# Every 64th (in the last stage every 32nd) gather of a graph kernel left out by GpSimd and fetched row by row from other queues

## What is computed

```python
h = relu(layernorm(x)); x = x + gcn(h)          # segment_sum(weight * (h W)[src], dst)
h = relu(layernorm(x)); x = x + hyperbolic(h)   # per edge: distance, 2-layer gate, h[col] * gate, segment_sum over row
h = relu(layernorm(x)); x = x + three attention layers(h)
    # e = leaky(alpha_s[src] + alpha_d[dst]); softmax over the edges of a node; segment_sum(h[src] * alpha, dst)
h = relu(layernorm(x)); x = x + two relational layers(h)
    # mean over the edges of each (dst, relation), times that relation's 64x64 matrix, summed
```

## Time and profile before

| | us |
|---|---|
| median of 3 runs | 17307.61 (17297.01 to 17308.78) |
| the profiled execution | 17330.74 |
| its span (first to last instruction) | 17329.0 |
| hyperbolic gathers, first to last start | 3252.8 to 5515.0 |
| attention gathers, three layers | 5779.3 to 12327.3 |
| last relational gathers | 15196.7 to 17296.0 |

### The profile page before, as it was taken

How to read it: one execution, slowest core, us unless ns; L and a number is a source line. 1 busy time by engine, 2 the same in 40 slices (tenths; PEclk the granted TensorE clock), 3 DMA queues, 4 the chain that set the end, 5 groups by cost and what they waited for, 6 DMA issues and landing times. The chain is left out here.

```text
span 17329.0 us, 347894 instructions
## 1 busy us (share of the span) xinstructions
PE 12031.7 (69%) x77017; PEld 8971.5 (52%) x77018; DVE 12499.8 (72%) x30848; ACT 7380.6 (43%) x19204; POOL 11519.1 (66%) x11855
## 2 busy tenths in 40 slices
PE   4443338599997577777777777777777888844444
PEld 2222225466665466665666666666546565533333
DVE  7777769777777788887888878888766666634443
ACT  1111129555554566665666656666441222300000
POOL 2777750377775577776777767777307777777777
PEclk7555555677776555555556555655696777755555
DMA  6333344333335222223222232222494666511111
GB/s 235 96 93 94 93 93 123 109 102 103 102 102 90 73 58 58 58 58 73 58 58 58 58 78 58 58 58 58 161 381 126 180 185 178 176 45 26 26 26 32
DMA packets 1329349, 1689.67 MB, mean 98 GB/s; under 512 B 835210, under 2 KB 903562, under 8 KB 1296591
## 3 DMA queue, kind: packets, MB, share of 16 engines
q1 hardware_dynamic: 899089, 875.57, 17.4%
q0 software_dynamic: 412640, 597.16, 15.7%
q10 hardware_dynamic: 17474, 215.22, 3.3%
HBM read 1072.24 MB, written 618.81 MB: 98 GB/s over the span
## 5 line engine op out<-in xcount | busy, mean ns | idle before, releaser
L2166 POOL DMA_INDIRECT gat_from_src<-gat_src_dram,gat_src_at x4992 | 4821.8, 966 | 1680.6 <-issue 1520.8
L3213 PE MATMUL rel_ps_sum<-all_node,rel_msg 128*64 128x128 f32 x6656 | 1413.5, 383 | 1501.4 <-DVEq L3172 1471.3
L3027 POOL DMA_INDIRECT rel_from_src<-typed_dram,rel_src_at x1664 | 1651.1, 992 | 1079.7 <-ACT rel_src_at L3042 596.7
L2387 PE MATMUL gat_ps_sum<-all_node,gat_msg 128*80 128x128 f32 x9984 | 2266.1, 420 | 42.3 <-DVE gat_msg L2281 7.9
L3213 PEld LDWEIGHTS rel_ps_sum<-all_node,rel_msg 128*64 128x64 f32 x6656 | 1133.8, 199 | 1979.2 <-DVEq L3172 1230.3
L1630 POOL DMA_INDIRECT all_node<-hyp_dst_dram,hyp_src_at x1768 | 1724.9, 976 | 603.0 <-issue 513.3
L2387 PEld LDWEIGHTS gat_ps_sum<-all_node,gat_msg 128*80 128x80 f32 x9984 | 2057.5, 252 | 102.3 <-issue 42.7
L3027 POOL DMA_INDIRECT rel_from_src<-typed_next_dram,rel_src_at x1664 | 1593.3, 958 | 566.2 <-issue 493.0
L1094 POOL DMA_INDIRECT bucket_dram<-all_node,order_index x1664 | 1616.0, 971 | 524.3 <-issue 505.8
L2329 DVE TENSOR_TENSOR again_sums_x<-again_sums_x,gat_ps_sum 80x128 f32 x4992 | 1393.1, 279 | 385.4 <-DVE again_sums_x L2329 213.0
L2291 DVE TENSOR_TENSOR_SCAN gat_ps_log<-gat_masks,gat_top,gat_ps_log 8x1024 f32<-8x1024 bf16 x624 | 1461.9, 2343 | 228.3 <-DVE again_sums_x L2329 220.4
(11 more groups left out here) (571 smaller groups left out, 26929.1 us busy)
## 6 DMA issues: line engine op xcount, KB each, us to landing
typed_dram<-typed_res SPq DMA_DIRECT2D x98, 2080.0 KB, 7.2
typed_next_dram<-rel_res ACTq DMA_DIRECT2D x98, 2080.0 KB
gat_relrow<-in_rows_dram SPq DMA_DIRECT2D x624, 256.0 KB
all_node<-gcn_table_dram SPq DMA_DIRECT2D x1664, 48.0 KB
gat_from_src<-gat_src_dram,gat_src_at POOLq DMA_INDIRECT x4992
bucket_dram<-by_dst_zero POOLq DMA_DIRECT2D x48, 1326.0 KB, 6.6
gsum_rec<-bucket_dram SPq DMA_DIRECT2D x221, 288.0 KB, 2.8
all_node<-lo_rows_dram SPq DMA_DIRECT2D x221, 256.0 KB
```

Of the source, the lines that this page charges most:

```text
L2166: nc.gpsimd.indirect_dma_start(from_src[:, q, k, :], None, g.gat_src[:, :], bass.IndirectOffsetOnAxis(ap=src_at[:, q, k:k + 1], axis=0)).t ...
L2387: last = nc.tensor.matmul(ps_sum[0:rows, k, :], msg[:, q % 2, k, :], member[:, q, k, :], start=True, stop=True)
L3027: nc.gpsimd.indirect_dma_start(from_src[:, q, k, :], None, table[:, :], bass.IndirectOffsetOnAxis(ap=src_at[:, q, k:k + 1], axis=0)).then_ ...
L3213: last = nc.tensor.matmul(ps_sum[0:D, k, :], msg[:, q % 2, k, :], member[:, q, k, :], start=True, stop=True)
```

## The change

**Which tiles.** In the three attention layers and the hyperbolic loop the eighth tile of every eighth chunk (one gather of 64), in the last relational layer the eighth tile of every fourth chunk (one of 32) is no longer gathered by GpSimd. It gathers seven tiles for these chunks. In the hyperbolic loop this is done for the 27 full groups of eight chunks. The first relational layer is as before.

**How they come instead.** SyncE reads 16 indices of that tile into registers (one TENSOR_LOAD, L211) and issues 16 one-row DMAs (L221) into a buffer `side` of 128 rows, once for each chunk, so that a group of eight chunks brings 128 rows. In the last layer a group has four chunks, and ScalarE issues 16 rows of each chunk beside the 16 of SyncE. At the last chunk of a group SyncE waits until all 128 rows have landed and the slot of the ring is free, and copies `side` into the ring with one DMA (`relay`). The next group's first fetch waits until that copy has landed, on ScalarE too. The consumers wait for it beside their seven gathers.

**With it.** The loops of SyncE, GpSimd and VectorE in attention and of all but TensorE in the hyperbolic stage are written for eight chunks instead of four (`eights`); the two mask loads of a chunk become one; the index rows for the fetches are loaded ahead of each loop (in the last layer converted by two VectorE copies of one partition, for which SyncE and ScalarE wait); in the stage of the GCN sums one transposition, one copy and two small stores make the index rows for the hyperbolic loop; in `typed_tables` TensorE waits for the weights after its first 25 transpositions and not before them.

The core of the diff:

```diff
+def fetch_piece(nc, eng, engine, rows, table, index, c, at, landed, top):
+    regs = bases(nc, engine, index, c, count=PIECE, per=PIECE, top=top)
+    for e, reg in enumerate(regs):
+        eng.dma_start(rows[at + e:at + e + 1, :], table[ds(reg, 1), :]).then_inc(landed, 16)
...
@@ edges_attention, SyncE (the hyperbolic loop: the same, without masks)
+                def relay(c, r, i):
+                    if r == GROUP - 1:
+                        for h in range(2):
+                            sp.wait_ge(side_in[h], 16 * (P // 2) * (i + 1))
+                            alone(sp, mark_s)
+                        sp.wait_ge(filled, free4(c))
+                        alone(sp, mark_s)
+                        sp.dma_start(from_src[:, r % 4, K - 1, :], side[:, :]).then_inc(side_out, 16)
+
+                def fetch(c, r, i):
+                    if r == 0 and not (isinstance(i, int) and i == 0):
+                        sp.wait_ge(side_out, 16 * i)
+                        alone(sp, mark_s)
+                    fetch_piece(nc, sp, ENG.SP, side, g.gat_src, single, c, r * PIECE, side_in[r // 4], N)
...
-                    for n, m in enumerate((g.first_mask, g.last_mask)):
-                        sp.dma_start(masks[:, q, n, :], m[ds(c * CE, CE)].partition_broadcast(H)
-                                     ).then_inc(mask_in[q], 16)
+                    sp.dma_start(masks[:, q, :, :], g.masks[:, ds(c * CE, CE)].partition_broadcast(H)).then_inc(mask_in[q], 16)
...
-                rounds(sp, [(load_rows, 4), (load_masks, 3)])
+                eights(sp, [(load_rows, 4), (load_masks, 3), (relay, 4), (fetch, 5)])
...
@@ edges_attention, GpSimd
-                    for k in range(K):
+                    for k in range(K if r < GROUP - 1 else K - 1):
...
@@ edges_attention, VectorE
-                    dve.wait_ge(got[q], 16 * K * (i + 1))
+                    dve.wait_ge(got[r], 16 * (K if r < GROUP - 1 else K - 1) * (i + 1))
+                    if r == GROUP - 1:
+                        dve.wait_ge(side_out, 16 * (i + 1))
...
@@ edges_relational, last layer
+                    rounds(sp, [(relay, 4), (fetch(sp, ENG.SP, 0, mark_s), 5)])
...
-                    for k in range(K):
+                    for k in range(K if first or q < 3 else K - 1):
...
-                    slotted(act, [(fields, 4), (activate, None, LAG)])
+                    act.wait_ge(single_c, 2)
+                    slotted(act, [(fields, 4), (fetch(act, ENG.Activation, 1, mark_a), 5), (activate, None, LAG)])
...
@@ typed_tables, TensorE
-                pe.wait_ge(w_in, 48)
...
                 pe.wait_ge(flips.row_kept, FLIPS)
+                pe.wait_ge(w_in, 48)
```

More of the change, by code:

```diff
@@ L55 @@
 ROW = 3 * P + 4
+PIECE = 16
+GROUP = P // PIECE
+SIDES = BCHUNKS // GROUP
 LAG = 16
@@ L146, in rounds, with eights, turn, in_fours @@
         turn(t, t // 4, t % 4)
+def eights(eng, steps, count=CHUNKS, full=None):
+    def turn(t, i, r):
+        for step, lead in steps:
+            if not isinstance(t, int) or 0 <= t + lead < count:
+                step(t + lead, (r + lead) % GROUP, i + (r + lead) // GROUP)
+    for t in range(-max(lead for _, lead in steps), 0):
+        turn(t, t // GROUP, t % GROUP)
+    full = (count - max(lead for _, lead in steps)) // GROUP if full is None else full
+    with eng.Fori(0, full) as i:
+        for r in range(GROUP):
+            turn(i * GROUP + r, i, r)
+    for t in range(GROUP * full, count):
+        turn(t, t // GROUP, t % GROUP)
+def in_fours(*steps):
+    def four(step):
+        return lambda c, r, i: step(c, r % 4, i * (GROUP // 4) + r // 4)
+    return [(four(step), lead) for step, lead in steps]
 def slotted(eng, steps, count=CHUNKS, slots=OWN_TILES):
@@ L328, in _ @@
                 sp.wait_ge(stored, 1)
-                for n, m in enumerate((g.first_mask, g.last_mask)):
+                for n in range(2):
+                    m = g.masks[n]
                     sp.dma_start(m[0:EP].rearrange("(g p e) -> p g e", p=P, e=P), mask[:, n, :, :]).then_inc(loaded, 16)
@@ L1414, in _ @@
                              ).then_inc(stored, 16)
-                sp.wait_ge(stored, 32)
+                sp.wait_ge(copied, len(tiles) + 1)
+                for h, row in enumerate(g.single_hyp):
+                    sp.dma_start(row.rearrange("o (j e) -> o j e", e=D), asides[0:SIDES, h * D:(h + 1) * D]).then_inc(stored, 16)
+                sp.wait_ge(stored, 64)
 def after_gcn(nc, g):
@@ L1619, in load, with gather @@
                     sp.dma_start(lorow[:, q % 2, :], g.lo_rows[ds(c * CE, CE)].partition_broadcast(P)).then_inc(lo_in[q], 16)
-                rounds(sp, [(load, 0)], BCHUNKS)
+                def relay(c, r, i):
[3 more added lines that the diff above has]
+                            alone(sp, mark_s)
+                        sp.wait_ge(joined, free4(c))
+                        alone(sp, mark_s)
+                        sp.wait_ge(h_kept, free4(c))
+                        alone(sp, mark_s)
+                        sp.dma_start(from_dst[:, r % 4, K - 1, :], side[:, :]).then_inc(side_out, 16)
+                def fetch(c, r, i):
+                    if isinstance(c, int) and c >= SIDES * GROUP:
+                        return
+                    if r == 0 and not (isinstance(i, int) and i == 0):
+                        sp.wait_ge(side_out, 16 * i)
+                        alone(sp, mark_s)
+                    fetch_piece(nc, sp, ENG.SP, side, g.hyp_dst, g.single_hyp[r * PIECE // D], i * GROUP // 2 + r % 4,
+                                r * PIECE, side_in[r // 4], N)
+                eights(sp, [*in_fours((load, 0)), (relay, 0), (fetch, 1)], BCHUNKS, full=SIDES - 1)
             @block.gpsimd
             def _(pool):
-                def gather(c, q, i):
+                def gather(c, r, i):
+                    q = r % 4
                     pool.wait_ge(joined, free4(c))
@@ L2980, in edges_relational, with fetch, step @@
             full, rest = N // P, N % P
+        def fetch(eng, engine, h, mark):
+            def step(c, q, i):
+                if q == 0 and not (isinstance(i, int) and i == 0):
+                    eng.wait_ge(side_out, 16 * i)
+                    alone(eng, mark)
+                fetch_piece(nc, eng, engine, side, table, single[h], c, h * D + q * PIECE, side_in[h][q // 2], top_row)
+            return step
         def place_of(engine, j, order, top):
@@ L3011, in _, with relay @@
                 else:
+                    for h in range(2):
+                        sp.dma_start(single[h].bitcast(F32).rearrange("o (c e) -> o c e", e=D),
+                                     g.tile_rows[:, h * D:(h + 1) * D].rearrange("(o c k) e -> o c k e", o=1, k=4 * K)[
+                                         :, :, 4 * K - 1, :]).then_inc(single_in, 16)
                     sp.dma_start(x[:, :, :], g.xs[:, :, :]).then_inc(x_in, 16)
+                    sp.wait_ge(single_c, 2)
+                    def relay(c, q, i):
+                        if q == 3:
+                            for landed in (*side_in[0], *side_in[1]):
+                                sp.wait_ge(landed, 16 * 2 * PIECE * (i + 1))
+                                alone(sp, mark_s)
+                            sp.wait_ge(filled, free4(c))
+                            alone(sp, mark_s)
+                            sp.dma_start(from_src[:, q, K - 1, :], side[:, :]).then_inc(side_out, 16)
+                    rounds(sp, [(relay, 4), (fetch(sp, ENG.SP, 0, mark_s), 5)])
                     sp.wait_ge(out_kept, START + OWN_TILES)
@@ L3149, in messages @@
                 def messages(c, q, i):
-                    dve.wait_ge(got[q], 16 * K * (i + 1))
+                    dve.wait_ge(got[q], 16 * (K if first or q < 3 else K - 1) * (i + 1))
+                    if not first and q == 3:
+                        dve.wait_ge(side_out, 16 * (i + 1))
                     dve.wait_ge(summed, half_ready(c, 1) - 4)
@@ L3185, in _ @@
                     dve.sem_inc(out_kept, START)
+                    dve.wait_ge(single_in, 32)
+                    for h in range(2):
+                        v.tensor_copy(single[h], single[h].bitcast(F32)).then_inc(single_c, 1)
                     dve.wait_ge(x_in, 16)
```

107 lines of the change are left out of this document (78 added, 29 removed).

## The result

The changed kernel takes **17252.1 us** (median of 9 runs, 17233.1 to 17269.5) against 17306.0 for the kernel before beside it (9 runs, 17296.0 to 17320.3): a ratio of 0.997, 95% interval 0.996 to 0.998, 54 us faster. The forecast was 17182 us, 126 us faster: right in sign, inside the range, and off by more than half of the gain. The profiled execution has a span of 17250.4 us, at its kernel's median, while the one shown for before lay 23 us above its own; so the two traces differ by 78.6 us where the medians differ by 54.

A forecast was written before the change was run, and what follows sets the result against it. GpSimd's gathers were taken to bound attention and the last stage, less surely the hyperbolic one. Attention -99, hyperbolic -35, last stage +8 and small parts 0 gave -126 us: 17307.6 to 17182 us, range 17090 to 17420.

The forecast's parts named there:

- Attention, -99 forecast: Attention layers: 78 gathers left out at 1.268 us each save 99 us, with GpSimd staying the bound.
- SyncE's sum of 76.8 us for a group: Attention: SyncE's rows, registers, loads, copy and landings take 76.8 us per eight chunks, against GpSimd's 79.9.
- a SyncE late by 10 us delays nobody, only its throughput counts: Attention: SyncE's waited-for signals come two chunks before their data are used, so 10 us of lateness costs nothing.
- Rival C: Attention: VectorE's longer loop fetches its code again each turn; three fetches make attention +265, 17546 us; chance 0.08.
- Hyperbolic, -35 forecast: Hyperbolic loop: 27 gathers left out at 1.280 us save 35 us; zero if TensorE's 91% is already its limit.
- Last stage, +8 forecast: Last relational layer: ScalarE takes over as bound at 40.5 us a group, +8 us instead of a 66 us gain.
- rival A: Last stage: ScalarE keeps up, so GpSimd stays the bound, -66 instead of +8, 17108 us; chance 0.30.
- half-difference of 0.027 us: Last stage: half the gap between ScalarE's 0.374 and SyncE's 0.320 us store, added to ScalarE's row, 0.48 us.
- Small parts, 0 forecast: Outside the main loops: `typed_tables` -14, last loop's start +10, hyperbolic index rows +2, attention starts +1 each; 0, within 15.
- The row price: SyncE's time per one-row DMA at a register address: 0.444 us, bounds 0.418 and 0.517.
- rival B: One-row issues cost as much as 128-partition ones, 0.517 us on SyncE and 0.571 on ScalarE: 18015 us; chance 0.19.
- the estimate of 0.464: Attention: a 72-float row, issued to 12 engines, might resemble the 8-partition mask load, 0.464 us in all.

The follow-up runs named there:

- Run 5: run 3 with SyncE fetching 8 of the 16 rows a chunk in attention, the other 64 edges getting fixed rows: 17148.9 us.
- run 3: The change with VectorE's attention loop and VectorE's and ScalarE's hyperbolic loops turning every four chunks instead of eight: 17217.5 us.
- run 7: run 6 with attention's 128 rows fetched in seven of a group's eight chunks, 17 to 19 rows each: 18327.8 us.
- run 9: run 6 with attention's 128 rows fetched in seven of a group's eight chunks, every register load of 16 as in the change: 17135.3 us.
- run 6: The change with VectorE's attention loop turning every four chunks and the hyperbolic stage as in the kernel before, without fetches: 17216.5 us.
- runs 4: The kernel before with VectorE's attention loop turning every eight chunks instead of four, nothing fetched or left out: 17320.6 us.
- Run 11: run 9 with VectorE's attention loop turning every eight chunks, as in the change: 17139.5 us.
- run 8: The kernel before with GpSimd gathering seven blocks a chunk in the hyperbolic stage, the eighth keeping 128 fixed rows: 17276.2 us.
- run 12: The kernel before with only the moved wait for the weights in `typed_tables`: 17292.3 us.
- runs 1: The kernel before with only the edits of `typed_tables` and the last relational stage; attention and hyperbolic stage untouched: 17228.8 us.

## Why the prediction was right in sign and wrong in size

**Attention, -99 forecast, +1 measured. The step that failed is SyncE's sum of 76.8 us for a group.** By the trace: rows 128 x 0.411 = 52.6 (I had 56.8), the rest of each chunk 8 x 2.49 = 19.9 (I had 16.8 for registers, destination and mask loads; the register load is 1.14, not 0.81, since I drew the price of a register from a load of eight on SyncE and one of one on ScalarE), 3.1 for the turn of the loop (I had put 0.8, and 2.5 to 2.8 of it is the code fetch), 3.0 for the copy and its landing (I had 2.4), and 1.4 for the rows that start later than that after the one before: 80.0 us; a whole turn in the third layer takes 80.4. That is above GpSimd's 79.9, so SyncE took the bound by a hair, and with it came the 7 to 9 us between the layers. I had the row itself too dear, what stands around it too cheap, and so the bound at the wrong engine: "a SyncE late by 10 us delays nobody, only its throughput counts" held inside the layers, and the throughput was what ran out; at the layers' ends the lateness was paid too. Run 5 (64 rows fewer, 60 us faster than run 3), run 7 (16 us more, 14 us a group) and run 9 (one landing hidden, 98 us faster than run 6) show it.

**Rival C stood beside the forecast with 0.08 and was a part of the cause.** Its mechanism came (2.7 to 2.9 us a turn at VectorE, where I had put 1.6 to 2.4), but I priced it at VectorE alone, whose slack takes it (runs 4 and 11), and left SyncE's own loop of 338 instructions out of the sum, although I named its length. Without its 2.5 us SyncE's turn would be some 78 us, under GpSimd's 79.9 (an estimate from the turn of 80.4); no run gives SyncE a short loop with all its rows, so how much of the loss is C's stays open. The earlier trace rows had only one of two instruction queues: q8 with 65 packets, the same in every run; q14 was left out, and it is the one that grew, to 9.86 MB, less than the tens of MB that I gave as C's sign. In the second layer of the change both came together: VectorE's hole delays the logits, TensorE gets them late, and L2402 waits again in the same turn, 6.6 us instead of 3.3, at 83.1 us a group. Run 11, with the long loop and 79.7 us in this layer, shows that the long loop alone does not do it; how the one wait makes the other, and that SyncE put VectorE there in this layer and not in the others, is argued from the waits, not tried.

**Hyperbolic, -35 forecast, about 0 measured. The step that failed is the choice between GpSimd and TensorE as the bound.** I wrote that it is zero if TensorE's 91% is already its limit; zero it was, and GpSimd is not what sets the pace (run 8, 81.9 us with 56 gathers). GpSimd's 1.280 us a gather, against 1.268 and 1.261 elsewhere, was the sign: eight of them took as long as the chunk did without it.

**Last stage, +8 forecast, -70 measured: rival A, with 0.30, was right.** The step that failed is the half-difference of 0.027 us for ScalarE's issue, taken from the stores of the earlier trace rows, and the price of the row itself: the issue takes 0.228 us on ScalarE and 0.225 on SyncE, and ScalarE's row in full takes 0.402, which is 64 x 0.078 = 5.0 us a group below my 0.48. GpSimd bounds as before, at 39.0 us for 31 gathers, within 0.1 of 31 x 1.261, and the sign that I gave for A, a GpSimd that never waits in this stage, came.

**Small parts, 0 forecast, within 1 us of it:** `typed_tables` -16 for -14, the last loop's start +12 for +10, the hyperbolic start +4 for +2. The first has some luck in it: run 12 gives -25 for the moved wait by itself, and the change's -16 also holds the late end of its last attention layer. Not forecast were the gaps between the attention layers, +9 and +7 for my +1 each, which belong to the late SyncE (runs 5 and 9 don't have them).

**The row price,** on which rival B stood with 0.19, came out at my lower bound (0.411, on average 0.424, against 0.418 and 0.517), so B did not come. By the Trainium skill ("DMA: Bandwidth & Descriptors", section "Why a DMA increments its semaphore by 16 and not by 1") a row of 72 floats goes to 12 engines and one of 64 to 16; they cost SyncE the same here (0.228 and 0.225 us), so the estimate of 0.464 found nothing to bear it out.

That the time fell inside the range was luck: errors of opposite sign hid each other, -70 instead of +8 in the last stage, +100 and +35 in the other two. These sizes are from one trace of each kernel, and stages with unchanged code differ by some 30 us between such traces (see the end); the signs don't hang on it.

## What to carry to other kernels

When work is moved to a queue that seemed free, add up that queue's whole turn, with the fetch of its own code, its register loads and each landing that it stands through, and treat a margin of a few per cent as none: here 76.8 against 79.9 us was 80.4 in truth. Before taking work from an engine, ask in each stage whether a busier one keeps the same time; a per-item time that is a little longer in one stage than in the others is a sign of it. If the moved work stalls, look for the one landing that the queue stands through and give it a slot without work: this change of the schedule alone turned -87 us (run 6) into -185 (run 9).

## What the runs showed of the hardware

- A loop whose turn has 360 to 490 instructions on VectorE or SyncE idles 2.4 to 3.1 us, rarely up to 4.5, at each branch back, and q14 moves more packets (81 before, 449 with VectorE's attention loop alone, 1204 in the change); turns of up to 236 instructions, and TensorE's of 480, do not. A turn of 290 on SyncE did in one layer and not in the two others (run 5). The rule of the Trainium skill named above speaks of this; the price is of these traces.
- A register load from SBUF on SyncE took 0.53 us or 0.69 (run 5) for 8 registers, 1.14 for 16, 1.37 for 17 and 1.79 for 19 when it started at a multiple of four indices, and 3.64, 3.84 and 4.05 for 17, 18 and 19 at other places.
- A one-row load at a register address is 0.225 to 0.228 us on SyncE and 0.228 on ScalarE; one follows the other after 0.41 us on SyncE and 0.38 on ScalarE.
- An unchanged stage differs from program to program: the first relational one took between 2149 and 2182 us, the gathers of the three attention layers between 6308 and 6340 us in the four programs that leave them as they were (the kernel before and runs 1, 8 and 12), the last stage between 2096 and 2126 us (before and runs 4, 8 and 12). Whether it is the program or the chip of the session is open. In a kernel of this size a difference of 20 to 30 us between two programs needs the trace of the stage that was changed, and more than one trace.
